# High and low part of the shared W2 in one product of 512 columns, summed by two operations of VectorE

## What is computed

```python
sh = gelu(jnp.einsum('nd,sdh->snh', xf, sw1) + sb1[:, None, :])      # S = 2, hidden 512
shared_out = (jnp.einsum('snh,shd->nd', sh, sw2) + sb2.sum(0)) / S   # the second layer
gates = xf @ router_w + router_b                                     # 8 experts, top 2
...
moe_out = jnp.einsum('ne,end->nd', comb, y)
return (shared_out + moe_out).reshape(B, L, D)
x = x + jnp.tanh(g_ffn[0]) * _L0_ffn_ref(...)
```

## Time and profile before

| | us |
|---|---|
| median of 3 runs | 381.22 |
| lowest and highest run | 380.16, 381.27 |
| span of the profiled execution, first to last instruction | 378.1 |
| PE busy | 370.8 |
| DVE busy | 282.0 |
| ACT busy | 241.7 |

### The profile page before, as it was taken

How to read it: one execution, slowest core, us unless ns; L and a number is a source line. 1 busy time by engine, 2 the same in 40 slices (tenths; PEclk the granted TensorE clock), 3 DMA queues, 4 the chain that set the end, 5 groups by cost and what they waited for, 6 DMA issues and landing times.

```text
span 378.1 us, 8799 instructions
## 1 busy us (share of the span) xinstructions
PE 370.8 (98%) x2773; PEld 352.3 (93%) x2774; DVE 282.0 (75%) x612; ACT 241.7 (64%) x540; POOL 221.4 (59%) x262
## 2 busy tenths in 40 slices
PE   8999999999999999999999999999999999999996
PEld 7898989999999989999999999999999997999995
DVE  5798799978988988799898897555556555554486
ACT  3666545665665545787878757766666665777850
POOL 8367657688878764377885226546565655653200
PEclk9999999999999999999999999999999999999999
DMA  7990000001000048511940022222223233650397
GB/s 219 313 340 6 2 14 29 16 21 35 14 14 14 29 142 333 222 32 14 300 138 2 14 46 84 80 63 85 83 79 89 85 84 111 210 144 30 110 350 251
DMA packets 33839, 40.15 MB, mean 106 GB/s; under 512 B 9674, under 2 KB 26508, under 8 KB 33676
## 3 DMA queue, kind: packets, MB, share of 16 engines
q1 hardware_dynamic: 28960, 29.40, 25.0%
q0 software_dynamic: 4768, 10.28, 8.9%
q10 hardware_dynamic: 76, 0.02, 0.0%
HBM read 27.88 MB, written 11.68 MB: 105 GB/s over the span
## 4 chain that ended last, share of the span: by engine, by line
PE 91%; DVE 2%; POOL 2%; issue 2%; DMA 1%; ACT 1%; DVEq 0%; POOLq 0%
PE psum L1336 12%; PE psum L1359 12%; PE psum L1296 10%; PE psum L1252 10%; PE psum L1504 8%; PE psum L1598 8%; PE psum L1478 6%; PE psum L1559 6%; PE psum L1219 3%; PE psum L1138 2%; PE psum L1176 2%; PE psum L1200 2%; PE psum L1583 2%; PE psum L1284 1%; PE psum L1491 1%
## 5 line engine op out<-in xcount | busy, mean ns | idle before, releaser
L743 POOL DMA_INDIRECT y_tok<-ysl,table x39 | 38.9, 996 | 41.7 <-ACT ysl L1029 36.5
L736 POOL DMA_INDIRECT xsl<-y_rows,table x39 | 38.7, 991 | 30.0 <-PE psum L1359 9.6
L709 POOL DMA_INDIRECT names<-named,pos x32 | 37.5, 1170 | 12.8 <-issue 7.9
L662 POOL TENSOR_TENSOR Eb<-Eb,rinv 128x512 f32<-128x512 f32 x32 | 33.5, 1065 | 13.1 <-DVE rinv L1810 13.1
L1073 ACT ACTIVATE hr<-psum,b_cur 128x256 f32<-128x256 f32 x48 | 20.1, 470 | 22.1 <-DVE b_cur L2103 12.3
L905 ACT ACTIVATE yTb<-psum 128x256 f32<-128x256 f32 x16 | 6.2, 385 | 42.7 <-PE psum L1316 42.7
L1598 PE MATMUL psum<-xsT_hi,w_cur 128*128 128x256 f32 x192 | 31.0, 284 | 0.0
L645 POOL TENSOR_TENSOR half_sum<-Eb 128x512 f32<-128x512 f32 x16 | 20.6, 1287 | 12.0 <-ACT Eb L860 11.8
L1598 PEld LDWEIGHTS psum<-xsT_hi,w_cur 128*128 128x128 f32 x192 | 26.5, 192 | 0.0
L2152 DVE TENSOR_TENSOR hr_lo<-hr,hr_hi 128x512 fp32r<-128x512 f32 x24 | 16.6, 692 | 13.2 <-ACT hr_hi L1086 13.0
L940 ACT ACTIVATE early_stage<-psum,vec_col 128x256 f32<-128x256 f32 x48 | 20.0, 467 | 8.8 <-PE psum L1336 8.0
(11 more groups left out here) (276 smaller groups left out, 1255.9 us busy)
## 6 DMA issues: line engine op xcount, KB each, us to landing
w_raw<-in_L_ffn_w SPq DMA_DIRECT2D x2, 4096.0 KB, 15.6
y_got<-y_tok SPq DMA_DIRECT2D x8, 512.0 KB, 8.3
xs_all<-in_x SPq DMA_DIRECT2D x4, 512.0 KB, 12.3
sw_raw<-in_L_ffn_sw SPq DMA_DIRECT2D x2, 1024.0 KB, 13.8
y_rows<-ybuf SPq DMA_DIRECT2D x16, 128.0 KB, 1.7
sw_lo_kept<-sw_lo SPq DMA_DIRECT2D x1, 2048.0 KB, 6.6
sw_lo<-sw_lo_kept SPq DMA_DIRECT2D x8, 256.0 KB, 3.1
out<-xs_all SPq DMA_DIRECT2D x3, 512.0 KB, 3.1
```

What stands on the lines that cost most here:

```text
L662: nc.gpsimd.tensor_tensor(Eb[q][:, heads, :], Eb[q][:, heads, :], rinv[:, q, heads].unsqueeze(2).broadcast_to([P, H // 2, CTX]), ALU.mult) ...
L709: nc.gpsimd.indirect_dma_start(names, bass.IndirectOffsetOnAxis(ap=pos[:, k, t:t + 1], axis=0), named[:, k, t, :], None).then_inc(scattere ...
L736: nc.gpsimd.indirect_dma_start(into[:, s % 2, :], None, y_rows, bass.IndirectOffsetOnAxis(ap=table[:, s, 0:1].bitcast(I32), axis=0)).then_ ...
L743: nc.gpsimd.indirect_dma_start(y_tok, bass.IndirectOffsetOnAxis(ap=table[:, s, 1:2].bitcast(I32), axis=0), ysl[:, s % 2, :], None).then_in ...
```

## The change

The two parts of W2, which lie 8192 words apart in each partition, get one view `sw2_both` that takes both. Where the hidden values' high part is the stationary operand, `products` now issues one product of 512 columns (256 of the high part of W2, 256 of the low part) into the whole bank, instead of two products of 256 columns into the same half. Where it is the low part, the product still has 256 columns and goes into the left half, as do the biases. The two halves are summed by DVE: each add of a tile is now two `scalar_tensor_tensor`, the second on the right half, and the second waits for the first by a new semaphore `half_added`, since both read and write the same row of `xs_all`.

```diff
+        sw_both = at_words("sw_both", [P, 2, 2 * SW_WORDS], AT_SW, F32R)
+        sw_s = [sw_both[:, i, :] for i in range(2)]
+        sw2_both = sw_both[:, :, SW_WORDS:].rearrange("p h (m n) -> p h m n", m=SHC)
...
                 def products(j, h_part, w_parts, start=False, stop=False, tiles=range(TPS)):
                     for t in tiles:
                         for m in (2 * j, 2 * j + 1):
-                            for w_part in w_parts:
-                                last = nc.tensor.matmul(bank[acc + t][:, 0:D], h_part[:, m, t * P:(t + 1) * P],
-                                                        w_part[:, m, :],
-                                                        start=start and m == 2 * j and w_part is w_parts[0],
-                                                        stop=stop and m == 2 * j + 1)
+                            last = nc.tensor.matmul(bank[acc + t][:, 0:w_parts * D], h_part[:, m, t * P:(t + 1) * P],
+                                                    sw2_both[:, 0:w_parts, m, :], start=start and m == 2 * j,
+                                                    stop=stop and m == 2 * j + 1)
...
-                    products(j, hT_h, sw2_s, start=(j == 0))
+                    products(j, hT_h, 2, start=(j == 0))
...
-                        products(j - 1, hT_l, sw2_s[0:1])
+                        products(j - 1, hT_l, 1)
...
                 nc.vector.scalar_tensor_tensor(row, bank[6 + t][:, 0:D], half_tg[:, 0:1], row, ALU.mult, ALU.add
+                                               ).then_inc(half_added, 1)
+                dve.wait_ge(half_added, c * TPS + (t + 1))
+                nc.vector.scalar_tensor_tensor(row, bank[6 + t][:, D:2 * D], half_tg[:, 0:1], row, ALU.mult, ALU.add
                                                ).then_inc(done, 1)
```

More of the change, by code:

```diff
@@ L130, in build @@
         sw_raw = at_words("sw_raw", [P, 2 * SW_WORDS], AT_SW + 2 * SW_WORDS)
-        sw_s = split("sw", [P, 2 * SW_WORDS], AT_SW, AT_SW + 2 * SW_WORDS)
+        sw_both = at_words("sw_both", [P, 2, 2 * SW_WORDS], AT_SW, F32R)
+        sw_s = [sw_both[:, i, :] for i in range(2)]
         w1_cur = at_words("w1_cur", [P, 2, 2, KD, HID], AT_SW + 2 * SW_WORDS, F32R)
+        sw2_both = sw_both[:, :, SW_WORDS:].rearrange("p h (m n) -> p h m n", m=SHC)
         sw1_s = [v[:, 0:SW_WORDS].rearrange("p (s k n) -> p s k n", s=S, k=KD) for v in sw_s]
@@ L315, in build @@
         bias_psum = sem("bias_psum")
-        out_ready, out_stored = sem("out_ready"), sem("out_stored")
+        half_added, out_ready, out_stored = sem("half_added"), sem("out_ready"), sem("out_stored")
         x_rows = x.rearrange("b (t p) d -> p (b t) d", p=P)
@@ L1392, in project @@
                         pe.wait_ge(sh_lo, c * PAIRS + j)
-                        products(j - 1, hT_l, sw2_s[0:1])
+                        products(j - 1, hT_l, 1)
                 pe.wait_ge(sh_lo, c * PAIRS + PAIRS)
-                products(PAIRS - 1, hT_l, sw2_s[0:1], stop=True)
+                products(PAIRS - 1, hT_l, 1, stop=True)
             def fold_all():
@@ L1426, in project_first @@
                 pe.wait_ge(sh_hi, j + 1)
-                products(j, hT_h, sw2_s, start=(j == 0), tiles=tiles)
+                products(j, hT_h, 2, start=(j == 0), tiles=tiles)
             def project_first_rest(j, tiles):
                 pe.wait_ge(sh_lo, j + 1)
-                products(j, hT_l, sw2_s[0:1], tiles=tiles)
+                products(j, hT_l, 1, tiles=tiles)
             products, hT_h, hT_l, _ = projection(early, ACC)
@@ L1443, in _ @@
                 pe.wait_ge(sh_lo, j + 1)
-                products(j, hT_l, sw2_s[0:1], stop=(j == PAIRS - 1))
+                products(j, hT_l, 1, stop=(j == PAIRS - 1))
             count_choices(1, bank[0][:, 0:COUNTS], bank[1][:, 0:COUNTS])
@@ L1518, in last_hi @@
                 pe.wait_ge(sh_hi, last_early * PAIRS + (j + 1))
-                return products(j, hT_h, sw2_s, start=(j == 0))
+                return products(j, hT_h, 2, start=(j == 0))
             def last_lo(j):
                 pe.wait_ge(sh_lo, last_early * PAIRS + (j + 1))
-                products(j, hT_l, sw2_s[0:1], stop=(j == PAIRS - 1))
+                products(j, hT_l, 1, stop=(j == PAIRS - 1))
             def last_early_sub():
@@ L2205, in add_last @@
                     dve.wait_ge(acc_psum, c * TPS + (t + 1))
-                    nc.vector.scalar_tensor_tensor(xs_all[:, c * TPS + t, :], bank[acc + t][:, 0:D], half_tg[:, 0:1],
-                                                   xs_all[:, c * TPS + t, :], ALU.mult, ALU.add).then_inc(out_ready, 1)
+                    row = xs_all[:, c * TPS + t, :]
+                    nc.vector.scalar_tensor_tensor(row, bank[acc + t][:, 0:D], half_tg[:, 0:1], row, ALU.mult, ALU.add
+                                                   ).then_inc(half_added, 1)
+                    dve.wait_ge(half_added, c * TPS + (t + 1))
+                    nc.vector.scalar_tensor_tensor(row, bank[acc + t][:, D:2 * D], half_tg[:, 0:1], row, ALU.mult, ALU.add
+                                                   ).then_inc(out_ready, 1)
             columns_rest(LAST, final)
```

## The result

| | before | after |
|---|---|---|
| median of the runs compared, us | 381.25 (4 runs, 380.16 to 381.51) | 385.33 (4 runs, 383.79 to 385.92) |
| ratio | | 1.0112, 95% interval 1.0087 to 1.0137 |
| span of the profiled execution, us | 378.1 | 383.6 |

The change makes the kernel 1.1% slower, 4.3 us by the ratio (3.3 to 5.2). The prediction was 385.4 us. A run is 1.7 us longer than its own span (385.29 beside 383.6 here, 380.13 beside 378.4 in a second profile of the kernel before), not 3: the spans of before are of executions quicker than the median. So the difference of spans, 5.2 to 5.5, is above the 4.3 of the ratio.

A forecast was written before the change was run, and what follows sets the result against it. PE was taken to bound the kernel nearly everywhere, DVE almost full at the end. Span 378.1 + 2.7 (stalls 3.33 less PE's 0.66) + 1.5 = 382.3 us; time 381.22 + 4.2 = 385.4 us, range 382.8 to 387.0.

The forecast's parts named there:

- PE's gain: Up to the last stage, products of 512 columns at 0.232 us replace pairs at 0.240, saving PE 0.66 us.
- DVE's cost: At each of eight handoffs, four half adds take 1.90 us in place of 0.88, 1.02 us more.
- Cheap wait: Rival: DVE's wait on itself is free, each handoff grows by only 0.80 us; 383.8 us, chance 0.16.
- The latency from DVE to PE: At handoffs, PE's product starts 0.15 us after DVE's result ends.
- The four stalls: In the shared stage, PE waits 1.16, 0.6, 0.85 and 0.72 us for DVE, 3.33 together.
- columns of 3: Before sub-block 3, DVE's list runs 2.04 us late, so PE waits 0.6 us for the hidden-value columns.
- DVE saturates: Rival: DVE's idle time in sub-blocks 2 and 3 doesn't absorb its lag, sub-block 4's stall grows; 386.6 us, chance 0.12.
- absorbed: Rival: ranking slack or the routed stage makes the stalls good, only the end counts; 382.1 us, chance 0.10.
- The routed stage runs from PE to PE and passes the shift on: After sub-block 5's add, the routed stage keeps the accumulated +2.7 us, with no term of its own.
- The end: In sub-blocks 6 and 7, DVE becomes the bound and the last adds end 1.5 us later.
- The last store follows as before: At the program's end, the last store follows the last adds unchanged, so their full +1.5 us reaches the span.
- Cheaper product: Rival: a product of 512 columns falls to 0.213 us and PE gains 3.5 us; 379.2 us, chance 0.04.

The follow-up runs named there:

- g2_products_only: Changed kernel without the second add of each tile (right halves left out of the sum), against the kernel before: ratio 1.0001 (0.9988 to 1.0014).
- g1_before: The kernel before, unchanged, run against itself for a second profile: ratio 1.0005 (0.9991 to 1.0019).

## Why the prediction came out right, point by point

**PE's gain: right.** The product costs 0.232 us as in attention. In g2_products_only the eight of sub-block 2 and the product behind them, 1.85 us later:

```profile
179.79 2.01 PE L1360 MATMUL psum<-sw_both,early_hT_hi 128*128 128x512 f32 x8
181.64 0.40 PE L1371 MATMUL psum<-bias_rows,bias_w 128*128 128x256 f32 x2
```

The shared stage of the products alone is 0.76 us shorter (predicted 0.66). Half of sub-block 0's share is lost, as predicted: from its first product to the first of sub-block 1 it is 7.26 us in g1_before and 7.21 in g2_products_only.

**DVE's cost: right.** 1.91 us for four, 1.66 to 1.67 more at the end for 1.62 predicted (1.5, and the 0.12 by which the add of 6 was to start earlier). "Cheap wait" falls with the 0.51 that stands at every second half. Its sum was also a little low: with a handoff 0.22 shorter, the stall of 0.85 at sub-block 4 becomes 0.46 to 0.63, not 0.35.

**The latency from DVE to PE: right in sum, wrong in its parts.** I took 0.15 us from the earlier trace rows. In after the product starts 0.06 after the add of sub-block 1, together with its weight load, but the product behind comes 0.10 later than without a wait (1.95 for 1.85): 0.16 in all. Behind the add of sub-block 5 the start is 0.22 later.

**The four stalls: right in place, sum 3.2 for 3.33.** Since idle times are too short, they are measured against g2_products_only, which has the same products and no stalls: from the last group before the wait to the one behind the first that waited (for the add of 5, to the first product, as in the table of stages):

| place | predicted | measured | idle time drawn |
|---|---|---|---|
| add of 1 | 1.16 | 1.05 | 0.80 |
| columns of 3 | 0.6 | 0.63 | 0.36 |
| add of 4 | 0.85 | 0.73 | 0.46 |
| add of 5 | 0.72 | 0.82 | 0.57 |

The columns, the third and the fourth, in after:

```profile
185.86 0.74 PE L1338 MATMUL psum<-early_cols_hi,sw_both 128*128 128x256 f32 x4 [0.36 <-DVE early_cols_lo L1854]
...
214.98 1.20 PE L1360 MATMUL psum<-sw_both,early_hT_hi 128*128 128x512 f32 x4 [0.46 <-DVE xs_all L1968]
...
230.80 0.76 PE L1478 MATMUL psum<-w_hi,hr_hi 128*128 x4 [0.57 <-issue]
```

From sub-block 3 to sub-block 4 nothing is lost (187.38 to 205.41 in after, 185.18 to 203.21 in g2_products_only, 18.03 us both): DVE's idle time did take up its lag, and "DVE saturates" falls. So does "absorbed". Net, the shared stage is 2.45 longer for 2.7 predicted.

**"The routed stage runs from PE to PE and passes the shift on": wrong.** It adds 1.3 us, in after mostly in two steps, one of them with a gather that lands late. I had no term for it, neither in the sum nor in a rival; "absorbed" had it making stalls good. The mark of this is that the products alone, a gain of 0.8 us by every row of the shared stage, give 1.0001 and 1.0009.

**The end: right for the first pair of adds, wrong for the last.** "The last store follows as before" was the failing step. Of the 1.5 us predicted, 0.90 is the later start of the sums (1.02 less the 0.12 of PE's gain), and there the rows have 1.04. The rest, the longer last pair of adds, costs nothing: the span ends 4.05 to 4.15 us after the issue of the group's store, which depends on the sums and not on the last adds. Net, the end is 1.07 longer.

**The sum.** The terms by the profiles are 2.45 + 1.30 + 1.66 - 0.59 = 4.8 against 4.2 predicted; the runs say 4.3 (3.3 to 5.2), which doesn't tell the two apart. The mechanism of the handoffs was right; that the forecast came so close was partly luck, because the missing loss of the routed stage and the two terms that were too large (2.7 for 2.45 and the end) go against each other. "Cheaper product" falls with the 0.232 us.

## What to carry to other kernels

Joining two products into one of twice the columns saved PE almost nothing here (0.231 us for 0.240); what it moves to VectorE is paid wherever VectorE's result is what PE waits for next, and moving one operation ahead only hands the lag to the next waiter. Find these handoffs by the margin, last use minus ready time, at each place, and compare it with what is added, even when PE waits nowhere now. Then measure a stall between the same two instructions of a kernel without it, and test a gain of PE by itself: here a gain of 0.8 us in one stage never reached the time. At the end of a program, look which transfer the end keeps its distance from: here it was the store before the last two, and an operation behind its issue was free.

## What was not expected of the hardware

- A VectorE operation of 0.48 us that waits for the one just issued starts 0.51 us after it, as predicted, where one that doesn't starts 0.40 after; new is that with one other operation between them the wait costs nothing (four halves in 1.66 us in place of 1.90).
- From VectorE's last add to TensorE's product behind it: 0.06 us, and 0.10 more until the products are at their usual distance; 0.22 at the first routed product.
- The span ended 4.05 to 4.15 us after the issue of the last group's store in all fourteen profiles, though the last add ended anywhere from 1.0 to 1.8 us after that issue.
- The same gather, issued at the same point of PE's work, landed after 3.0 us in one kernel and 4.7 in another, and the routed stage was 0.7 to 1.7 us longer in all seven profiles in which PE comes to it later or earlier than before. The cause stays open.
